# First chunk of a macaron FFN–attention–FFN kernel: GpSimd's root moved ahead of a weight piece, the turned weights in two banks by halves, the guard of the sums as a last column

## The chip, the cores and the metric

The kernel runs on one core of one Trainium2 chip. Its time is the device time of one execution in microseconds (us). The kernel before took 542.42 us (median of 3 runs, 542.03 to 543.43).

## The reference

The input x has 2048 tokens of 128 numbers. The layer is a "macaron": half a mixture-of-experts FFN, attention, and half an FFN again, with the same FFN weights both times.

```python
def _L0_attn_ref(x, Wq, Wk, Wv):              # D = 128
    q, k, v = x @ Wq, x @ Wk, x @ Wv
    score = softmax(q @ k.T, axis=-1) / sqrt(128)
    return score @ v

def _L0_ffn_ref(x, centroids, expert_biases, Ws_up, Ws_down, W_up, W_down):
    xf = x.reshape(T, D)                      # T = 2048, E = 64 experts, F = 64, TOP_K = 8
    shared = silu(xf @ Ws_up) @ Ws_down
    aff = xf @ centroids.T
    _, idx = top_k(aff + expert_biases, TOP_K)
    w = sigmoid(aff[idx])
    w = w / (sum(w, axis=-1) + 1e-08)         # the 1e-08 is the "guard" of the sums
    cw = zeros((T, E)).at[tokens, idx].add(w)
    h = silu(einsum('td,edf->etf', xf, W_up))
    y = einsum('etf,efd->etd', h, W_down)
    return shared + einsum('etd,te->td', y, cw)

x = x + 0.5 * ffn(layernorm(x));  x = x + attn(layernorm(x));  x = x + 0.5 * ffn(layernorm(x))
```

## The kernel before

Tokens are worked on in four chunks of 512 (`CH`), in each of the two FFNs; the chunk's number n runs from 0 to 7, and n = 0 is the first chunk of the first FFN. Every expert is computed for every token, two experts at a time: a chunk has 33 units, unit 0 (the shared expert) and units 1 to 32 (a pair of experts each, 128 hidden numbers).

A unit passes through the engines in this order. TensorE (PE) computes the hidden rows (`up`, L1201, three matmuls L1197 to L1199, since each fp32 operand is kept as a high and a low part). ScalarE (ACT) applies silu (L458). VectorE (DVE) multiplies by the gate, which is the token's weight for that expert spread over 64 partitions (`gate_unit`, L739). ACT makes the high part (L469), DVE or GpSimd (POOL) the low part (L296). PE multiplies by the down weights and accumulates (`down`, L1228, three matmuls L1239 to L1241), five units behind `up` (`LAG`).

The gates reach the partitions in two ways. Units 7 to 32 of chunk 0 get them by DMA: the turned weights are copied to the tile `gates` (L503), stored to memory (L335, queue of SyncE, SP), and read back with a broadcast, two DMAs of 128 KB to each unit (L358). Units 1 to 6 (`EARLY`) of the chunks 0 and 4 get them by a matmul with a selection matrix `sel` (`spread_gate`, L1226) from the turned weights `cwT`, since the store and the read back would come too late.

Before its first unit the first chunk needs its whole prologue: statistics, normalised tokens turned, affinities, the eight largest, sigmoid, the sum with its guard (`pro_sum`, L944), the reciprocal, the weights `cw2` (`first_weights`, L930), four transposes into one PSUM bank `mp` (`pro_cw`, L1325, matmuls L1302), and the copy of that bank to `cwT` (L597). PE fills two of its waits there with matmuls that nobody reads (`stay_awake`, L1415, L1418).

The expert weights arrive as 16 pieces (`raw`, L327), alternately of the up and the down weights. ACT makes the high part of a piece (`piece_hi`, L548, cast L550) and POOL the low part (`piece_lo`, L385, subtraction L387). All of this stands in written order: each engine's instructions run strictly in the order in which the program lists them, and wait for each other by semaphores; no scheduler moves them.

The next chunk's prologue runs inside a chunk. Of chunk 1's, POOL computes the inverse square root of the variances (`rstd`, L378: L382 and a power, L383) in chunk 0's unit 3, behind the pieces 3 and 4. DVE refines it (L773, L760 to L762), normalises the tokens in two pairs of tiles (L776, units 5 and 6), and PE turns them (L1309, unit 8).

The buffers: `hid` is four banks of `lrow`; `bank` is four banks, of which `mp` is the third and `mq` the fourth; `yacc` (the accumulator of `down`) is the first bank in even chunks.

## Time and profile before

| | us |
|---|---|
| median of 3 runs (lowest, highest) | 542.42 (542.03, 543.43) |
| the profiled execution's own time | 542.28 |
| its span (first to last instruction) | 540.5 |
| PE busy in the span | 532.0 |
| ACT, DVE, POOL busy | 406.6, 408.8, 272.6 |

The profiled execution is one of many; its span leaves out some 1.8 us at the two ends of it. The page gives busy times and the chain of work that ended last; further views of the same trace give the instructions in order of time, one engine at a time, the busy times in stretches, and for each group of DMAs the time from issue to landing. Times on the axis are us from the span's start. "[idle before <-X]" behind an instruction is how long its engine had nothing to do ahead of it, and what ended this. Matmuls are pipelined: a 128x512 one is shown as 0.40 us, but the next one starts 0.23 us behind it.

### The profile page before, as it was taken

Reading aid. Unit: us, or ns where it says so; the run is one execution under the profiler, and the core shown is the slowest. Engines: PE = TensorE matmul, PEld = TensorE weight load, DVE = VectorE, ACT = ScalarE, POOL = GpSimd, SP = SyncE. Lnnn points to the kernel's source line nnn. Section 1 sums busy time; section 2 is a strip of 40 time slices with the busy share of each in tenths; the row PEclk is TensorE's granted clock in tenths of the full one; section 3 lists DMA queues with packets and bytes.
Section 4 is the critical chain, followed back from the end, with each engine's and each line's share of the span. In section 5 each row is a group of like instructions: output and inputs, shape, how many; then the busy total and the mean of one; then the engine's idle time right before and its main releaser. Section 6 shows DMA issues by size and latency. Waiting matters only on the chain.

```text
span 540.5 us, 8719 instructions
## 1 busy us (share of the span) xinstructions
PE 532.0 (98%) x2710; PEld 437.2 (81%) x2710; DVE 408.8 (76%) x934; ACT 406.6 (75%) x815; POOL 272.6 (50%) x241
## 2 busy tenths in 40 slices
PE   8899999999999999999999999999999999999997
PEld 6577887887788888799999999878887888788886
DVE  6888679877975677867877889779668767965664
ACT  7798778877887775866666657778779777877773
POOL 2679657775776764000000000267576676766663
PEclk9999999999999999999999999999999999999999
DMA  8477564564566550000000000165565565657652
GB/s 270 137 228 217 180 203 161 178 198 149 174 191 195 183 172 1 2 1 0 1 2 1 2 1 0 44 193 169 168 198 165 168 201 166 187 156 204 204 191 84
DMA packets 44494, 72.25 MB, mean 134 GB/s; under 512 B 8864, under 2 KB 9888, under 8 KB 44448
## 3 DMA queue, kind: packets, MB, share of 16 engines
q1 hardware_dynamic: 44000, 71.37, 42.6%
q8 instruction: 21, 0.34, 0.3%
q10 hardware_dynamic: 448, 0.33, 0.2%
q14 instruction: 25, 0.20, 0.1%
HBM read 69.57 MB, written 2.10 MB: 133 GB/s over the span
## 4 chain that ended last, share of the span: by engine, by line
PE 89%; DVE 4%; ACT 2%; DMA 1%; issue 1%; POOL 1%; SPq 0%; DVEq 0%
PE lrow L1197 13%; PE lrow L1198 13%; PE lrow L1199 13%; PE bank L1239 10%; PE bank L1241 10%; PE bank L1240 10%; PE bank L1302 6%; PE bank L1526 3%; PE bank L1527 3%; PE bank L1528 3%; DMA wide<-gates_dram 1%; DVE pmax L982 1%; PE bank L1309 1%; DVE gpart_lo L296 1%; PE bank L1198 1%
## 5 line engine op out<-in xcount | busy, mean ns | idle before, releaser
L296 POOL TENSOR_TENSOR gpart_lo<-gated,gpart_hi 128x512 fp32r<-128x512 f32 x174 | 223.7, 1296 | 163.2 <-ACT gpart_hi L469 161.6
L458 ACT ACTIVATE lrow<-lrow 128x512 f32<-128x512 f32 (+1 forms) x245 | 143.8, 587 | 62.5 <-PE lrow L1199 62.0
L739 DVE TENSOR_TENSOR gated<-lrow,wide 128x512 f32<-128x512 f32 x170 | 116.2, 684 | 56.9 <-ACT lrow L458 53.4
L469 ACT CAST gpart_hi<-gated 128x512 fp32r<-128x512 f32 x174 | 106.6, 613 | 6.0 <-DVE gated L739 5.4
L1239 PE MATMUL bank<-gpart_lo,wdn_hi 128*128 128x512 f32 x246 | 97.8, 397 | 0.0
L1241 PE MATMUL bank<-gpart_hi,wdn_hi 128*128 128x512 f32 x246 | 97.7, 397 | 0.0
L1240 PE MATMUL bank<-gpart_hi,wdn_lo 128*128 128x512 f32 x246 | 97.2, 395 | 0.0
L739 DVE TENSOR_TENSOR lrow<-lrow,wide 128x512 f32<-128x512 f32 x74 | 51.5, 696 | 26.9 <-ACT lrow L458 26.9
L1115 DVE TENSOR_TENSOR pT_lo<-bank,pT_hi 128x512 fp32r<-128x512 f32 x64 | 43.7, 684 | 21.7 <-ACT pT_hi L671 21.7
L296 DVE TENSOR_TENSOR gpart_lo<-lrow,gpart_hi 128x512 fp32r<-128x512 f32 (+1 forms) x83 | 56.6, 682 | 1.5 <-ACT gpart_hi L469 1.3
L671 ACT CAST pT_hi<-bank 128x512 fp32r<-128x512 f32 x64 | 38.0, 594 | 24.2 <-PE bank L1302 24.0
L469 ACT CAST gpart_hi<-lrow 128x512 fp32r<-128x512 f32 (+1 forms) x83 | 49.1, 592 | 8.4 <-DVE lrow L739 8.2
L1239 PEld LDWEIGHTS bank<-gpart_lo,wdn_hi 128*128 128x128 f32 x246 | 46.2, 188 | 11.3
L1241 PEld LDWEIGHTS bank<-gpart_hi,wdn_hi 128*128 128x128 f32 x246 | 46.2, 188 | 11.1
L1240 PEld LDWEIGHTS bank<-gpart_hi,wdn_lo 128*128 128x128 f32 x246 | 46.2, 188 | 10.9
L664 ACT ACTIVATE prow<-lrow,nmax 128x512 f32<-128x512 f32 x63 | 43.6, 695 | 14.2 <-DVE nmax L987 14.2
L1197 PE MATMUL lrow<-xnT_lo_a,wup_hi 128*128 128x512 f32 x128 | 52.1, 407 | 1.2 <-DVE gpart_lo L296 0.6
L1197 PE MATMUL lrow<-xnT_lo_b,wup_hi 128*128 128x512 f32 x128 | 51.3, 401 | 0.2 <-DVE gpart_lo L296 0.2
L1199 PE MATMUL lrow<-xnT_hi_a,wup_hi 128*128 128x512 f32 x128 | 50.7, 396 | 0.0
L1198 PE MATMUL lrow<-xnT_hi_b,wup_lo 128*128 128x512 f32 x128 | 50.7, 396 | 0.0
L1198 PE MATMUL lrow<-xnT_hi_a,wup_lo 128*128 128x512 f32 x128 | 50.6, 395 | 0.0
L1199 PE MATMUL lrow<-xnT_hi_b,wup_hi 128*128 128x512 f32 x128 | 50.1, 392 | 0.0
(280 smaller groups left out, 977.3 us busy)
## 6 DMA issues: line engine op xcount, KB each, us to landing
wide<-gates_dram SPq DMA_DIRECT2D x488, 128.0 KB, 3.0
raw<-in_w_up SPq DMA_DIRECT2D x8, 256.0 KB, 4.8
raw<-in_w_down SPq DMA_DIRECT2D x8, 256.0 KB, 5.0
gates_dram<-gates SPq DMA_DIRECT2D x8, 128.0 KB, 2.2
x<-in_x SPq DMA_DIRECT2D x3, 256.0 KB, 4.5
out_dram<-x SPq DMA_DIRECT2D x3, 256.0 KB, 2.9
x<-in_x SPq DMA_DIRECT2D x1, 128.0 KB, 2.8
x<-in_x ACTq DMA_DIRECT2D x1, 128.0 KB, 3.0
```

Source lines behind the costliest of these rows:

```text
L296: return eng.tensor_tensor(gpart[1][0:m, U % NGP, :], gated_at(U)[0:m, :], gpart[0][0:m, U % NGP, :].bitcast(F32), ALU.subtract)
L458: nc.scalar.activation(dst[0:m, :], hid[U % NH][0:m, :], ACT.Silu).then_inc(s_silu, 1)
L469: nc.scalar.copy(gpart[0][0:m, U % NGP, :], gated_at(U)[0:m, :]).then_inc(s_ghi, 1)
L664: nc.scalar.activation(prow[:, j * CH:(j + 1) * CH], logit_bank(t, j), ACT.Exp, bias=nmax[:, t % 2:t % 2 + 1], accum_out=psums[:, t, j:j + ...
L739: nc.vector.tensor_tensor(gated_at(U), a, b, ALU.mult).then_inc(s_gated, 1)
L1115: nc.vector.tensor_tensor(pT[1][at], tb[q % 2][:, :].rearrange("p (k n) -> p k n", n=P), pT[0][at].bitcast(F32), ALU.subtract).then_inc(a_ ...
L1197: nc.tensor.matmul(out, a[0], b[1], start=True, stop=False)
L1198: nc.tensor.matmul(out, a[1], b[0], start=False, stop=False)
L1199: return nc.tensor.matmul(out, a[0], b[0], start=False, stop=True)
L1239: nc.tensor.matmul(y, w[0], g[1], start=(U % (NCH * PAIRS + 1) == 0), stop=False)
L1240: nc.tensor.matmul(y, w[1], g[0], start=False, stop=False)
L1241: nc.tensor.matmul(y, w[0], g[0], start=False, stop=(u == (UNITS - 1 if n % NCH < NCH - 1 else UNITS - LAG - 1))).then_inc(s_down, 1)
```

## The change

There are five edits, nearly all of them for chunk 0.

- POOL's `rstd` for chunk 1 moves from unit 3 to unit 0, ahead of weight piece 3 (the fourth) instead of behind the pieces 3 and 4.
- ACT's cast of weight piece 0 moves ahead of `make_sel` and of the cast of the shared down weights.
- The weights tile `rec` gets a 65th column in each of its four groups, set to 1e-8 once; the sum runs over 65 columns, and the addition of the guard (L948) is gone, in all eight chunks.
- Chunk 0's turned weights go to two banks, two transposes each (`mp` and `bank[0]`, columns 0 to 255). ACT copies the halves apart, with a semaphore of its own for the first, and PE's matmul of unit 1's gate runs in two halves, each behind its own copy. The copy to `gates` is in halves, too.
- The first `down`, which writes `bank[0]`, waits for the copy to `gates`. The wait for the whole of `cwT` ahead of chunk 0's unit loop goes, as the halves' waits stand in `spread_gate`.

```diff
--- before.py
+++ after.py
@@ -111,7 +111,8 @@
         stat = sb("stat", [P, 2, TPC, 6])
         mv = sb("mv", [P, 2, TPC, 2])
         rs = sb("rs", [P, 2, 4, TPC])
-        rec = sb("rec", [P, TPC, E])
+        rec_guard = sb("rec_guard", [P, TPC, E + 1])
+        rec = rec_guard[:, :, 0:E]
         sil = sb("sil", [P, TPC, E])
         rest = sb("rest", [P, TPC, E])
         top = sb("top", [P, TPC, TOP])
@@ -157,6 +158,7 @@
         s_x0b = sem("x_in0_second_half")
         s_small, s_sdn, s_value, s_qk, s_bias = (
             sem("small_in"), sem("shared_down_in"), sem("value_in"), sem("qk_in"), sem("bias_in"))
+        f_cwT, f_cwr = sem("first_cwT_half"), sem("first_cwT_half_read")
         s_eps, s_zero = sem("eps_made"), sem("cw_zeroed")
         j_out, j_aff, j_silu, j_hi, j_lo = (sem("shared_" + n) for n in ("and_aff", "aff_copied", "silu", "hi", "lo"))
         p_rec = sem("p_reciprocal")
@@ -410,6 +412,7 @@
                                     base=0, pattern=[[-1, P]], channel_multiplier=1).then_inc(s_id, 1)
             nc.gpsimd.memset(wsdn_pad[0:F, :].bitcast(F32), 0.0).then_inc(s_pad, 1)
             nc.gpsimd.memset(cw2[:, :, E:2 * E], 0.0).then_inc(s_zero, 1)
+            nc.gpsimd.memset(rec_guard[:, :, E:E + 1], 1e-8).then_inc(s_zero, 1)
             link(nc.gpsimd.memset(mhalf[:, :], -0.5))
             pool.wait_ge(s_small, 16 * 2)
             nc.gpsimd.tensor_copy(small[0][:, 0:E + F], raws[:, 0:E + F]).then_inc(s_wh0, 1)
@@ -426,10 +429,12 @@
                     for u in range(min(c, 1), UNITS):
                         if on_pool(place(u, n)):
                             low_part(nc.gpsimd, place(u, n)).then_inc(s_glop, 1)
+                        if n == 0 and u == 0:
+                            rstd(0, 1, p_st, p_rs)
                         if n == 0 and u % 2 == 0 and PRE + u // 2 < 2 * WP:
                             piece_lo(PRE + u // 2)
                         if c + 1 < NCH:
-                            if u == 3:
+                            if n and u == 3:
                                 rstd(0, n + 1, p_st, p_rs)
                             if u == 18:
                                 weights(n + 1)
@@ -500,7 +505,11 @@
                     nc.scalar.copy(cwT[:, :], mp[:, :]).then_inc(p_cwr, 1)
                 if n:
                     act.wait_ge(s_gout, 16 * n)
-                nc.scalar.copy(gates[:, :], mp[0:E, :]).then_inc(s_gates, 1)
+                if n:
+                    nc.scalar.copy(gates[:, :], mp[0:E, :]).then_inc(s_gates, 1)
+                else:
+                    nc.scalar.copy(gates[:, 0:GW], mp[0:E, 0:GW])
+                    nc.scalar.copy(gates[:, GW:CH], bank[0][0:E, 0:GW]).then_inc(s_gates, 1)
 
             def epi_y(n):
                 act.wait_ge(s_down, place(PAIRS, n) + 1)
@@ -580,11 +589,11 @@
                         if f == 0:
                             first_hi(0)
                             first_hi(1)
+                            piece_hi(0)
                             act.wait_ge(s_spread, 1)
                             make_sel()
                             act.wait_ge(s_sdn, 16 * 2)
                             nc.scalar.copy(wsdn[0][:, :], rawd[:, :]).then_inc(s_wh, 1)
-                            piece_hi(0)
                             piece_hi(1)
                             first_sil(0)
                             first_sil(1)
@@ -593,8 +602,9 @@
                             silu_unit(1, n)
                             hi_unit(0, n)
                             silu_unit(2, n)
-                            act.wait_ge(p_cwT, 1)
-                            nc.scalar.copy(cwT[:, :], mp[:, :]).then_inc(p_cwr, 1)
+                            for h in range(2):
+                                act.wait_ge((f_cwT, p_cwT)[h], 1)
+                                nc.scalar.copy(cwT[:, h * GW:(h + 1) * GW], (mp, bank[0])[h][:, 0:GW]).then_inc((f_cwr, p_cwr)[h], 1)
                             piece_hi(2)
                             silu_unit(3, n)
                             hi_unit(1, n)
@@ -944,9 +954,8 @@
             def pro_sum(n):
                 dve.wait_ge(p_w, n + 1)
                 total = (mp if n else bank[0])[:, TPC * E:TPC * E + TPC] if n != NCH else wsum[:, 0, :]
-                link(nc.vector.tensor_reduce(total, rec[:, :, :], AX, ALU.add))
-                link(nc.vector.tensor_scalar(wsum[:, 0, :], total, 1e-8, None, ALU.add))
-                nc.vector.reciprocal(inverse_sum(n), wsum[:, 0, :]).then_inc(p_inv, 1)
+                link(nc.vector.tensor_reduce(total, rec_guard[:, :, :], AX, ALU.add))
+                nc.vector.reciprocal(inverse_sum(n), total).then_inc(p_inv, 1)
 
             def epi_x(n, c):
                 dve.wait_ge(e_yT, n + 1)
@@ -1013,7 +1022,7 @@
                             first_lo(1)
                             first_top()
                             first_chosen()
-                            dve.wait_ge(s_zero, 1)
+                            dve.wait_ge(s_zero, 2)
                             first_weights(n)
                             small_lo(1, wsdn, rawd, 0, D)
                             lo_unit(0, n)
@@ -1223,6 +1232,13 @@
                     if u == EARLY and n:
                         pe.wait_ge(a_x, NQ)
                     one = sel[:, u - 1, :, :].rearrange("p e f -> p (e f)")
+                    if n == 0 and u == 1:
+                        for h in range(2):
+                            pe.wait_ge((f_cwr, p_cwr)[h], 1)
+                            half = slice(h * GW, (h + 1) * GW)
+                            ins = nc.tensor.matmul(gate_bank(u, n)[:, half], one, cwT[:, half], start=True, stop=True)
+                        ins.then_inc(s_gate, 1)
+                        return
                     nc.tensor.matmul(gate_bank(u, n), one, cwT[:, :], start=True, stop=True).then_inc(s_gate, 1)
 
             def down(u, n):
@@ -1232,6 +1248,7 @@
                     pe.wait_ge(s_w, 2 * ((u - 1) // (PAIRS // WP)) + 2)
                 if U == 0:
                     pe.wait_ge(s_wl, 2)
+                    pe.wait_ge(s_gates, 1)
                 wait_low(pe, U)
                 w = [a[:, u - 1, :] for a in wdn] if u else [a[0:F, :] for a in wsdn]
                 g = [a[0:m, U % NGP, :] for a in gpart]
@@ -1324,7 +1341,13 @@
 
             def pro_cw(n):
                 pe.wait_ge(p_cw, n + 1)
-                if n % NCH == 0:
+                if n == 0:
+                    for i in range(TPC):
+                        h, at = i // GT, i % GT * P
+                        ins = nc.tensor.transpose((mp, bank[0])[h][:, at:at + P], flat(cw2)[:, i * P:(i + 1) * P], ident[:, :])
+                        if i % GT == GT - 1:
+                            ins.then_inc((f_cwT, p_cwT)[h], 1)
+                elif n == NCH:
                     turn(flat(cw2), mp, p_cwT)
                 else:
                     for i in range(TPC):
@@ -1432,8 +1455,8 @@
                         stay_awake(2)
                         pro_cw(n)
                         stay_awake(1)
-                    if c == 0:
-                        pe.wait_ge(p_cwr, f + 1)
+                    if n == NCH:
+                        pe.wait_ge(p_cwr, 2)
                     for u in range(LEADS[1] if n == NCH else min(c, 1), UNITS):
                         if u <= EARLY and (c or u >= LEADS[f]):
                             up(u, n)
```

GpSimd's (POOL's) order in chunk 0, from the low part of weight piece 0 to that of piece 4; `wup_lo` and `wdn_lo` are low parts of weight pieces, `rs` is the root of the next chunk. Before:

```order
L387 TENSOR_TENSOR wup_lo<-raw,wup_hi 128x512
L387 TENSOR_TENSOR wdn_lo<-raw,wdn_hi 128x512
L387 TENSOR_TENSOR wup_lo<-raw,wup_hi 128x512
L387 TENSOR_TENSOR wdn_lo<-raw,wdn_hi 128x512
L387 TENSOR_TENSOR wup_lo<-raw,wup_hi 128x512
L382 TENSOR_SCALAR rs<-mv 128x4
L383 TENSOR_TENSOR rs<-rs,mhalf 128x4
```

And now:

```order
L389 TENSOR_TENSOR wup_lo<-raw,wup_hi 128x512
L389 TENSOR_TENSOR wdn_lo<-raw,wdn_hi 128x512
L389 TENSOR_TENSOR wup_lo<-raw,wup_hi 128x512
L384 TENSOR_SCALAR rs<-mv 128x4
L385 TENSOR_TENSOR rs<-rs,mhalf 128x4
L389 TENSOR_TENSOR wdn_lo<-raw,wdn_hi 128x512
L389 TENSOR_TENSOR wup_lo<-raw,wup_hi 128x512
```

The two instructions of the root moved ahead of two pieces.

ScalarE's (ACT's) order from the first high parts of the turned tokens to the copy to `gates`. Before:

```order
L566 CAST xnT_hi_a<-bank 128x256 x2
L555 CAST sel<-spread 128x768
L586 CAST wsdn_hi<-rawd 128x128
L550 CAST wup_hi<-raw 128x512
...
L458 ACTIVATE wide<-lrow 128x512
L597 CAST cwT<-bank 128x512
L550 CAST wup_hi<-raw 128x512
L458 ACTIVATE wide<-lrow 128x512
L469 CAST gpart_hi<-lrow 128x512
L503 COPY gates<-bank 64x512
```

And now:

```order
L575 CAST xnT_hi_a<-bank 128x256 x2
L559 CAST wup_hi<-raw 128x512
L564 CAST sel<-spread 128x768
L596 CAST wsdn_hi<-rawd 128x128
...
L463 ACTIVATE wide<-lrow 128x512
L607 CAST cwT<-bank 128x256 x2
L559 CAST wup_hi<-raw 128x512
L463 ACTIVATE wide<-lrow 128x512
L474 CAST gpart_hi<-lrow 128x512
L511 COPY gates<-bank 64x256
L512 COPY gates<-bank 64x256
```

The cast of the first weight piece moved up by two instructions, and the copies to `cwT` and to `gates` became two of half the columns each.

VectorE's (DVE's) order in chunk 0 from the chosen weights to the tile `cw` that PE turns. Before:

```order
L921 SCALAR_TENSOR_TENSOR rec<-rest,sil 128x256
L947 TENSOR_REDUCE bank<-rec 128x4
L948 TENSOR_SCALAR wsum<-bank 128x4
L949 RECIPROCAL bank<-wsum 128x4
L936 TENSOR_TENSOR rest<-rec,bank 128x4x12
```

And now:

```order
L931 SCALAR_TENSOR_TENSOR rec_guard<-rest,sil 128x4x64
L957 TENSOR_REDUCE bank<-rec_guard 128x4
L958 RECIPROCAL bank<-bank 128x4
L946 TENSOR_TENSOR rest<-rec_guard,bank 128x4x12
```

One instruction between the sum and the reciprocal is gone.

## Rows read from the trace of the kernel before

**Rows 1.** The page, part 1: busy us, share of the span, instructions

```profile
PE 532.0 (98%) x2710; PEld 437.2 (81%) x2710; DVE 408.8 (76%) x934; ACT 406.6 (75%) x815; POOL 272.6 (50%) x241
```

**Rows 2.** Stretches: length, each engine's busy us, clock, DMA share, GB/s

```profile
15.10:25.60 10.50, 8.59 (x33) 5.39 (x31) 9.04 (x24) 8.41 (x17) 7.50 (x7) 1.00 0.47 128
25.60:34.70 9.10, 9.10 (x41) 7.02 (x42) 7.22 (x12) 8.51 (x17) 7.41 (x6) 1.00 0.91 239
34.70:46.10 11.40, 10.99 (x48) 7.98 (x47) 11.27 (x30) 10.24 (x20) 8.57 (x8) 1.00 0.65 211
60.00:540.00 480.00, 476.68 (x2481) 396.29 (x2479) 361.31 (x809) 355.99 (x718) 233.40 (x199) 1.00 0.40 125
```

**Rows 3.** The chain that ended last, chunk 0: start us, us, what

```profile
8.80 1.30 POOL wup_lo L387
...
21.28 1.05 POOL rs L383
...
29.51 5.06 DMA wide<-gates_dram
```

**Rows 4.** ACT in order of time: start us, us, instruction, count, idle before

```profile
6.53 0.74 ACT L566 CAST xnT_hi_a<-bank 128x256 fp32r<-128x256 f32 x2
7.16 0.83 ACT L555 CAST sel<-spread 128x768 fp32r<-128x768 f32 x1
...
13.85 0.58 ACT L597 CAST cwT<-bank 128x512 fp32r<-128x512 f32 x1 [0.76 <-PE bank L1302]
...
16.33 0.58 ACT L503 COPY gates<-bank 64x512 f32<-64x512 f32 x1
```

**Rows 5.** L327 up to 12 us, twelve weight pieces: issue to landing

```profile
DMA to landing us min/median/max: 3.6/5.7/6.1
```

**Rows 6.** PE in order of time, 10 to 15 us

```profile
10.14 0.50 PE L1197 MATMUL lrow<-xnT_lo_a,wup_hi 128*128 128x512 f32 x1 [0.43 <-POOL wup_lo L387]
...
12.35 1.03 PE L1418 MATMUL bank<-ident 128*128 128x256 f32 x4
13.21 0.60 PE L1302 MATMUL bank<-ident,cw 128*128 128x128 f32 x4
...
14.49 0.50 PE L1226 MATMUL bank<-cwT,sel 128*128 128x512 f32 x1 [0.24 <-ACT cwT L597]
```

**Rows 7.** DVE in order of time, 11 to 16 us

```profile
11.71 0.16 DVE L948 TENSOR_SCALAR wsum<-bank 128x4 f32<-128x4 f32 x1
...
12.70 0.21 DVE L938 TENSOR_TENSOR cw<-cw,rest 128x48 f32<-128x48 f32 x1
...
15.12 0.69 DVE L739 TENSOR_TENSOR lrow<-wide,bank 128x512 f32<-128x512 f32 x1 [0.64 <-PE bank L1226]
```

**Rows 8.** DVE and PE in order of time, around chunk 1's normalised tokens

```profile
17.08 0.37 DVE L1029 BATCH_NORM_AGGREGATE mv<-stat 128x2 f32<-128x6 f32 x4
...
20.52 0.69 DVE L296 TENSOR_TENSOR gpart_lo<-lrow,gpart_hi 128x512 fp32r<-128x512 f32 x1
22.36 0.17 DVE L773 TENSOR_SCALAR bank<-mv 128x4 f32<-128x4 f32 x1 [1.15 <-POOL rs L383]
...
25.59 0.63 PE L1309 MATMUL bank<-ident,xn_a 128*128 128x128 f32 x4 [1.48 <-issue]
```

**Rows 9.** SP's store of the gates, and DVE at unit 13

```profile
16.94 0.51 SPq L335 DMA_DIRECT2D gates_dram<-gates  x1
...
34.66 0.69 DVE L739 TENSOR_TENSOR gated<-lrow,wide 128x512 f32<-128x512 f32 x1 [0.82 <-DMA wide<-gates_dram]
```

**Rows 10.** Issue to landing: eight of L358 from 22.95 on; the one at 29.51

```profile
DMA to landing us min/median/max: 3.4/3.7/3.9
...
DMA to landing us min/median/max: 5.1/5.1/5.1
```

**Rows 11.** DMA queues from 31.6 to 31.8 us: packets, MB, share of 16 engines

```profile
q8 instruction: 1, 0.02, 34.4%
```

**Rows 12.** PE in order of time, unit 17 of chunk 0

```profile
39.72 0.50 PE L1197 MATMUL lrow<-xnT_lo_a,wup_hi 128*128 128x512 f32 x1 [0.22 <-DVE gpart_lo L296]
```

## The prediction

> **What bounds the kernel now.** I read the page's busy times first: PE is busy 532.0 of 540.5 us [rows 1], so all that any edit can win is in PE's few gaps. The busy times by stretch say where they are: from 60 us on PE is busy 476.68 of 480.00, while from 15.1 to 25.6 it is busy 8.59 of 10.50 [rows 2]. The gaps that the change can reach are all in chunk 0's first 46 us. In that stretch the chain of waits, read third, goes from one engine to the next: POOL's low part of weight piece 0 at 8.80, the root for chunk 1 at 21.28, and from 29.51 a DMA of 5.06 us that brings the gates of unit 13 [rows 3]. Behind it DVE is the bound: from 34.7 to 46.1 it is busy 11.27 of 11.40 [rows 2], and PE waits for it, as at unit 18's `up` at 39.72 [rows 12]. So there are two sections with different limits: up to about 26 us the engines' own order, then the stream of gates, whose landing at 34.57 sets DVE free at 34.66 after an idle time of 0.82 [rows 9]. What is won ahead of 26 us counts only as far as this stream comes sooner too. That is the question of this case.
>
> **Part 1, weight piece 0 sooner.** ACT's cast of it takes the place of `sel` at 7.16 [rows 4] instead of coming two casts later; POOL's subtraction now starts at 8.80 [rows 3], the cast's end plus 0.07. The piece, issued at 2.58, landed 3.6 later at 6.2, the quickest of the twelve issued together [rows 5], so the cast finds its data. It and POOL come about 0.9 sooner. PE's first `up` matmul of unit 1 stands at 10.14 behind an idle time of 0.43 [rows 6]; with the step of 0.23 from the matmul before it and its start-up it could have stood at about 9.55. I take 0.59 for PE's own queue: the filler matmuls start at 11.76 instead of 12.35, and end 0.86 later at 12.62 [rows 6]. This alone gains nothing at 14.49; it only takes PE's filler out of the way of the transposes, which stood at 13.21 [rows 6] though `cw` was complete at 12.70 + 0.21 = 12.91 [rows 7].
>
> **Part 2, the guard.** L948 takes 0.16 and its place in the row 0.20 (11.71 to the reciprocal behind it) [rows 7]. The sum's row becomes 65 columns long, 4 of 256 elements more; I take nothing. `cw` is complete at 12.71. With PE free the transposes start about 0.1 later, at 12.83, instead of 13.21: a gain of 0.38 that needs both parts. The other seven L948 lie beside a PE that doesn't wait for them, and I take nothing; if one were on the path, it would be 0.20. The column stride of 65 instead of 64 changes reads that already ran in four groups; bound 0 to 0.05 each, taken 0.
>
> **Part 3, the halves.** The four transposes are shown as 0.60, two of them as about 0.38, so the first half can be copied at 12.83 + 0.38 + 0.04 = 13.25. Two 256-column casts take 0.74 as a pair against 0.58 for one of 512 [rows 4], so both are done at about 13.99 instead of 13.85 + 0.58 = 14.43. PE's second half of the gate starts at about 14.04 against 14.49, and being half as long ends 0.1 sooner still: unit 1's gating on DVE starts at about 14.57 instead of 15.12 [rows 7], a gain of 0.55. The cover is there: ACT sat idle 0.76 ahead of the copy [rows 4], and the filler behind the transposes ends before 14.04. The new wait of the first `down` for the copy to `gates` has behind it all of PE's queue, but PE gets there only after the gate of unit 5, which waits for DVE's gating of unit 3, and this stands behind the statistics of 17.08 [rows 8], now at about 16.9; the copy ends at about 16.5. Cost nothing.
>
> **Part 4, the copy to `gates`.** It follows the high part of unit 1, 0.55 sooner, and costs 0.16 more as two halves (0.74 against 0.58 again). The store, issued at 16.94 [rows 9], leaves at about 16.94 - 0.55 + 0.16 = 16.55. Gain 0.4.
>
> **Part 5, the root.** DVE's statistics end at 17.08 + 0.37 [rows 8], now some 0.55 sooner; POOL then needs 1.3 us for both instructions and is done at about 18.2, not 22.3. Nothing in POOL's queue behind it is late: the high part of piece 3 is the third instruction behind the copy to `gates` in ACT's queue, 16.33 + 3 x 0.48 + 0.62 = 18.4 by [rows 4], now 18.0, and finds POOL free at about 18.2. DVE had waited 1.15 for the root at 22.36 [rows 8]. Now it gets to L773 right behind its low part (20.52 + 0.69) [rows 8], and this is fed by ACT, 0.4 sooner: 20.8 instead of 22.36. PE's transposes of chunk 1's tokens follow by the same 1.55: 24.05 instead of 25.59 [rows 8]. So at 26 us the engines are 1.5 ahead.
>
> **Part 6, what is late next.** SP's stream of gates starts when the store has landed, and up to unit 13 no engine holds it: a unit's slot is free once the unit six before it is gated. It is 14 DMAs of 128 KB and 4 weight pieces of 256 KB long up to unit 13. From 25.6 to 34.7 the DMA engines are busy 0.91 of the time [rows 2]. So this stream comes 0.4 sooner, not 1.5. Its last DMA of unit 13 took 5.1 us, where the eight issued from 22.95 on took 3.4 to 3.9 [rows 10]; in this time an instruction fetch of 16 KB took a third of the 16 engines' 0.2 us, so 1.1 us of one of them [rows 11]. PE has the most instructions, so I take it for PE's; it then moves ahead with PE by some 1.3. It falls on the landing of unit 12 instead of 13, and its queue still carries most of the delay to unit 13. From this I take 0.1 more: unit 13 lands at about 34.07, and DVE, PE and the rest follow by 0.5. The other 1.0 is DVE waiting for gates in units 9 to 13.
>
> **The sum.** 0.55 - 0.16 + 0.1 = 0.5 us. The profiled execution would go from 542.28 to 541.8. The median of the runs shown is 0.14 above that execution: 542.42 - 0.5 = 541.9.
>
> **A rule weighed.** Behind `rec`, every tile declared later moves by 32 bytes in the partition, as the new tile has 1040 bytes and takes 1056; the tile `wide`, into which the gates are read back, moves from an address of 32 past a multiple of 64 to a multiple of 256. The Trainium skill (DMA: Bandwidth & Descriptors, How a descriptor splits into AXI transactions) says that a descriptor which doesn't start on a 256-byte boundary fetches from the boundary below it. By an estimate from this page a 2048-byte row of before would cost 71 beats of 32 bytes against 64 now, if the rule holds for the written side as well. No run here shows it yet.
>
> **The rivals.**
> A, the stream lets go. If unit 13 lands with 3.9 us like its forerunners, because the fetch falls elsewhere or the transfers of 128 KB get shorter with the tile's new address, it lands at 29.51 - 0.4 + 3.9 = 33.0, and DVE's idle 0.82 [rows 9] shows that it would have been ready at 33.84 and now at about 32.6 to 33. The gain is then 1.2 to 1.5 us, at the most the 1.55 of part 5: 540.9 to 541.2. For it: the 5.1 stands alone among its kind [rows 10]. Against it: DMA share 0.91 [rows 2], and the issues themselves are only 0.4 sooner. The rule of the Trainium skill above would work this way.
> B, nothing arrives. If the halves cost ACT more than they bring (each 0.37 and a wait), the store leaves where it left, and the stream with it. The gain of parts 1 to 3 and 5 is then all spent waiting for gates: 542.4.
> C, slower. The cast of weight piece 0 now stands ahead of `sel`, of the casts of the shared weights and piece 1, of the sigmoid and of a table load. If its transfer lands late, ACT stands. It has 1.0 us of room (6.2 against 7.16). Of the twelve weight pieces the slowest took 6.1 [rows 5]; with 6.1 here the cast starts at 8.7, 1.5 late, and the silus and the copy of `cwT` behind the table load come 1.5 later, less the 0.76 that ACT had idle [rows 4]. The gates leave 0.7 later instead of 0.4 sooner: 543.1. It decides from a landing of about 4.6 us on.
> That the change doesn't do what it says I see in none of its parts.
>
> **Chances.** The forecast 0.62 (own range 541.5 to 542.3), A 0.18, B 0.13, C 0.07. A measurement of this kernel tells about 0.3% from no change, 1.6 us: faster means below 540.8, slower above 544.0. Only the far end of A with some luck of the runs reaches below 540.8; I give it 0.10. Above 544.0 only C with a much later landing, 0.03. The rest, 0.87, is within. The range takes in the near end of A and most of C's, with the runs' own scatter of 542.03 to 543.43: 540.9 to 542.9.
>
> **What would show it.** Right: the four transposes of the weights from about 12.8, unit 1's gating at 14.6, the store at 16.55, DVE's L773 at 20.8 with no wait for the root, PE's transposes of chunk 1 at about 24.1, and in units 9 to 13 DVE waits for gates of 1.5 to 2 us in sum, where it had 0.82. Behind 46 us both kernels run alike, 0.5 apart. Wrong: if DVE waits less than 0.8 for gates up to unit 13, A is the case; if the store leaves at 16.9 or later, B; if ACT has a gap ahead of weight piece 0, C. If the two traces differ by more than a few tenths behind 60 us, something that I took at nothing (the stride, the addresses) isn't.

## The result and the profile after

The changed kernel takes 539.4 us in the median of 4 runs (538.99 to 539.7), the kernel before 542.22 in the same comparison. The ratio is 0.9943, with a 95% interval of 0.9926 to 0.996: faster by 0.6%. I had said 541.9 and 540.9 to 542.9, and gave a gain of over 0.3% a chance of one in ten. The profiled execution took 539.49 with a span of 537.7, 2.8 less than before.

The busy times of the page after, against [rows 1]:

```profile
PE 530.3 (99%) x2711; PEld 437.8 (81%) x2711; DVE 407.2 (76%) x926; ACT 407.1 (76%) x817; POOL 272.3 (51%) x242
```

The stretches after, columns as in [rows 2]:

```profile
15.10:25.60 10.50, 9.75 (x40) 6.39 (x39) 10.12 (x26) 9.32 (x20) 7.60 (x8) 1.00 0.46 148
25.60:34.70 9.10, 9.10 (x42) 7.02 (x40) 6.18 (x10) 8.35 (x17) 7.20 (x6) 1.00 0.72 221
34.70:46.10 11.40, 10.28 (x42) 7.26 (x41) 11.27 (x30) 10.10 (x20) 8.85 (x8) 1.00 0.68 212
60.00:540.00 480.00, 473.81 (x2477) 395.47 (x2475) 359.97 (x802) 356.12 (x717) 232.26 (x198) 1.00 0.39 124
```

From 15.1 to 25.6 PE works 1.16 us more than in [rows 2]; from 25.6 to 34.7 DVE works 1.04 less, since it waits. The last row is the surprise: 473.81 against the 476.68 of [rows 2], 2.87 less, though at 60 us PE is only 0.8 ahead and has no gap behind it to lose. The window's last 2.3 us lie behind the end of the changed kernel.

To find where the 2.8 us arise I set each matmul of the one trace against the same matmul of the other. The changed kernel is ahead by 0.31 us at the transposes of the weights, 0.52 at 15.06, 1.72 at 25.59, 1.34 at 36.5, 0.80 at 46.0 and 0.81 at 60. Then it gains steadily: 1.04 at 137, 1.29 at 207, 1.43 at 368, 1.92 at 431, 2.44 at 489, 2.80 at 531. So 0.8 us come from chunk 0 and 2.0 from stretches that the edited lines don't touch.

The first 26 us went as forecast. PE after, in order of time, against [rows 6] and [rows 8]:

```profile
11.76 1.03 PE L1441 MATMUL bank<-ident 128*128 128x256 f32 x4
12.90 0.66 PE L1347 MATMUL bank<-ident,cw 128*128 128x128 f32 x4
13.39 0.60 PE L1441 MATMUL bank<-ident 128*128 128x256 f32 x2
13.89 0.57 PE L1239 MATMUL bank<-cwT,sel 128*128 128x256 f32 x2
...
23.87 0.63 PE L1326 MATMUL bank<-ident,xn_a 128*128 128x128 f32 x4 [0.31 <-issue]
```

ACT after, against [rows 4], and the queue of SP, against [rows 9]:

```profile
7.33 0.62 ACT L559 CAST wup_hi<-raw 128x512 fp32r<-128x512 f32 x1
...
13.37 0.65 ACT L607 CAST cwT<-bank 128x256 fp32r<-128x256 f32 x2 [0.15 <-PE bank L1347]
...
15.81 0.36 ACT L511 COPY gates<-bank 64x256 f32<-64x256 f32 x1
16.07 0.37 ACT L512 COPY gates<-bank 64x256 f32<-64x256 f32 x1
16.47 0.51 SPq L337 DMA_DIRECT2D gates_dram<-gates  x1
```

DVE after, against [rows 7 to 9]:

```profile
12.64 0.21 DVE L948 TENSOR_TENSOR cw<-cw,rest 128x48 f32<-128x48 f32 x1
...
14.60 1.29 DVE L749 TENSOR_TENSOR lrow<-wide,bank 128x512 f32<-128x512 f32 x2 [0.18 <-PE bank L1239]
...
20.66 0.15 DVE L783 TENSOR_SCALAR bank<-mv 128x4 f32<-128x4 f32 x1
...
33.85 0.69 DVE L749 TENSOR_TENSOR gated<-lrow,wide 128x512 f32<-128x512 f32 x1 [1.40 <-DMA wide<-gates_dram]
```

The first gating of a unit with a gate starts at 14.60, the store leaves at 16.47, and the wait for the root (1.15 at 22.36 in [rows 8]) is gone. What was won is then spent waiting for gates. The waits of DVE up to 46 us (sum, times, longest), and the two transfers in the chain, which answer to the one in [rows 3]:

```profile
DVE gated L749 <- DMA wide<-gates_dram: 2.9, 3, 1.4
```
```profile
22.85 3.37 DMA wide<-gates_dram
...
28.91 4.85 DMA wide<-gates_dram
```

### The profile page after: what moved, and what is told of

It is laid out like the page before. It is cut to its first block, busy times and chain, and to the rows that moved or that the text cites. A ratio compares the mean times of both kernels' runs of the same rounds, so it can differ in the third digit from the quotient of the medians.

```text
span 537.7 us, 8716 instructions
## 1 busy us (share of the span) xinstructions
PE 530.3 (99%) x2711; PEld 437.8 (81%) x2711; DVE 407.2 (76%) x926; ACT 407.1 (76%) x817; POOL 272.3 (51%) x242
## 4 chain that ended last, share of the span: by engine, by line
PE 88%; DVE 5%; ACT 2%; DMA 2%; issue 1%; POOL 1%; POOLq 0%; DVEq 0%; SPq 0%; ACTq 0%
PE lrow L1206 12%; PE lrow L1208 12%; PE lrow L1207 12%; PE bank L1256 10%; PE bank L1258 10%; PE bank L1257 10%; PE bank L1319 5%; PE bank L1549 3%; PE bank L1551 3%; PE bank L1550 3%; DMA wide<-gates_dram 2%; PE bank L1441 1%; POOL gpart_lo L298 1%; DVE gpart_lo L298 1%; DVE pmax L991 1%
```

## Experiments on the part that nobody edited

Two theories at first: the new tile `rec_guard` is 32 bytes longer and shifts every tile declared behind it, and that speeds up the steady stretches; or something in the new code does. Times are medians; each ratio is to runs of the kernel before on the same chip (542.0 to 542.6 in all studies). An "interval" is the mean time from the start of a matmul to the start of the next in one profile, over pairs that stand side by side in both traces, gaps over 260 ns left out: 46 to 190 us is the first FFN, 190 to 340 attention, 340 to 515 the end of attention and the second FFN. Before they are 221.5, 138.0 and 216.2 ns, after 220.8, 137.8 and 214.5. (From 355 us on, without the end of attention, the last figure would be 223.1 before and 221.2 after.)

**Only the shift.** `+ sb("pad", [P, 8])` behind `rec` in the kernel before.

> The kernel before, with an unused tile of 32 bytes declared behind rec: no instruction is added, removed or moved, only every tile declared later stands 32 bytes further, as in the changed kernel. What is measured of the change is 2.8 us, of which PE shows 0.8 at 46 us and the rest growing steadily through the two FFNs (0.43 us between 46 and 190, 1.34 between 355 and 515), with no gap of PE getting shorter. Theory Addresses: the steady part comes from the tiles' addresses; this kernel then gains about 2.0 us (540.2), with nothing won ahead of 46 us but perhaps some tenths in the stream of gates. Theory Phase (the steady part comes from the order in which the engines meet, which the edits of chunk 0 have shifted): this kernel stays within 0.3 us of before (542.2).

Measured: 540.33 (539.48 to 540.99), ratio 0.9964 (0.9952 to 0.9977). The profile is 1.96 us ahead at 531 us, and 0.04 behind at 60. The code as it was, with the shift alone, gives the steady part.

**Only the code.** The changed kernel with 224 unused bytes more, so that the tiles start as before modulo 256.

> The changed kernel with an unused tile of 224 bytes behind the guarded tile, so that every later tile stands 256 bytes further than in the kernel before and has the same remainder modulo 256 as there. Theory Addresses: it keeps what is won ahead of 46 us, 0.8, and loses the steady part of 2.0: 541.4. Theory Phase: it keeps all, 539.4.

Measured: 541.76 (540.34 to 542.51, 11 runs), ratio 0.9986 (0.9976 to 0.9997); no drift behind 60 us (0.22 behind the kernel before at 60, 0.24 at 531). So the shift is the cause, and the theory of the new code falls. By the median the edited code alone is worth some 0.1%, and the forecast of 0.5 us lies in the interval; its profiled execution, with 542.51 the slowest of the eleven, shows none of it at 46 us.

**Which tile.** One or two unused tiles ahead of `wide`, `xnT_a` or `gpart` bring some to a multiple of 256 and leave those ahead of them. Within the FFN the tiles behind a second one (all behind `wide` in the first kernel, `gpart` in the last) don't start as before, though: their start is the same modulo 64, but modulo 256 it is 32 instead of 224.

```
wide only:        + sb("pad", [P, 8], F32, ffn)    ahead of wide, and again behind it
all but wide:     + the same behind wide; + sb("pad_b", [P, 8]) ahead of pT
gpart only:       + the same ahead of gpart, and again behind it
all but gpart:    + the same ahead of xnT_a, and again ahead of gpart
```

> The kernel before with 32 bytes ahead of the tile wide and 32 behind it: wide, into which SyncE's DMAs read the gates back, starts at a multiple of 256 bytes, and every later tile of the FFN stays at 32 past a multiple of 64, as before. Theory Written side: the gain of the 32 bytes (1.8 us of the kernel before in the first study) comes from the DMAs' writes into wide, whose 2048-byte rows no longer straddle a 64-byte line at both ends; this kernel then has all of it, 540.3. Theory Read side (tiles that PE, DVE and ScalarE read and write, gpart above all): it has none, 542.1.

> The counterpart: wide stays where it was (32 past a multiple of 64), and the 32 bytes stand behind it, so that the turned tokens, gated, gpart and all the rest of the FFN, and the attention's tiles, start at multiples of 256. Theory Written side: no gain, 542.1. Theory Read side: all of it, 540.3. If both kernels have a part, the tiles share the effect.

Measured: with `wide` alone 541.71, ratio 1.0 (0.9991 to 1.0009); with all but `wide` 540.48, ratio 0.9971 (0.996 to 0.9981). The target of the DMAs doesn't matter. With that falls the rule of the Trainium skill (DMA: Bandwidth & Descriptors, How a descriptor splits into AXI transactions) as an explanation here: the rows of `wide` then begin at a multiple of 256 bytes, and no time is won. This kernel isn't a clean test, since `xnT_a` and `gpart` moved by 64 bytes (intervals 222.2 and 215.4); the clean one is its counterpart, which has the gain without `wide`.

> The kernel before, in which only gpart_hi and gpart_lo (the moving operands of the matmuls with wdn) begin at a multiple of 256 bytes; every other tile of the FFN keeps a start of 32 modulo 64, and so do pT and its neighbours. Theory G (what counts are the starts of the moving operands that TensorE streams all the time): 540.3 to 540.8, a steady interval between matmuls in the second FFN near 214.5 ns against 216.2. Theory D (what counts are the tiles that VectorE, ScalarE and GpSimd read and write, gated above all, since gated goes with every second unit): 541.9 to 542.2, interval 216.2 ns. Theory S (each tile has its share): 541.2 to 541.6.

> The complement: xnT_a, xn_a, biased_a, aff_a, gated, yT and xn2 begin at a multiple of 256 bytes, gpart_hi and gpart_lo at 32 modulo 256 (as every tile before was 32 modulo 64). Theory G: 541.9 to 542.2, no gain in the second FFN, where the only moving operands besides gpart are xnT_b, which did not move. Theory D: 540.3 to 540.8. Theory S: 541.2 to 541.6.

Measured: `gpart` alone 540.77, ratio 0.9973 (0.9961 to 0.9984), intervals 221.6, 137.9, 214.7; all but `gpart` 541.25, ratio 0.9978 (0.9969 to 0.9987), intervals 220.8, 137.9, 215.6. So the second FFN goes by `gpart` nearly alone and the first by a tile from `xnT_a` to `xn2`. By the totals the first fits Theory G (540.3 to 540.8) and the second Theory S (541.2 to 541.6), so none of the three holds for both; by stage the split is sharper than any of them said: where `gpart` is what moves, the second FFN's interval falls by 1.5 ns also for the `up` matmuls that read `xnT_b`, which didn't move (230.3 against 233.5 for the low part of the weights). So the start of one operand also shows in the matmuls beside it in PE's row. What none of the theories explains: in the first FFN, where the same `gpart` is read as often, its start changed nothing (221.6 with it alone moved; 220.8 with the others moved, whether it stood at 0 or at 32).

**Which start.** 96, 160 and 224 unused bytes behind `rec`, in place of 32.

> The kernel before with 96 bytes behind rec instead of 32: wide and all behind it start at a multiple of 64, but not of 256 (64 past it). If the boundary that counts is 64 bytes, the gain is that of 32 bytes, 540.3. If it is 256 bytes, as the Trainium skill's rule on descriptors (DMA: Bandwidth & Descriptors, How a descriptor splits into AXI transactions) would have it, there is no gain or a small one, 541.7 to 542.1.

> The kernel before with 160 unused bytes behind rec: all tiles behind it (xnT_a, gated, gpart, pT) begin at 128 modulo 256. So far the steady interval between matmuls went with the start of the tile that TensorE reads: in the first FFN by xnT_a's start 220.8 ns at 0, 221.5 at 64, 222.2 at 32, 221.5 at 224; in the second FFN by gpart's 214.5 at 0, 215.2 at 64, 215.5 at 32, 216.2 at 224; in attention by pT's 137.8 at 0, 136.6 at 64, 137.9 at 224. Theory 1 (the start modulo 128 or 64 decides, and 128 does as 0 does): 540.3, intervals 220.8, 214.5, 137.8. Theory 2 (the place relative to other operands decides, so that each start modulo 256 or more has a value of its own): any total from 539.8 to 542.2, and intervals that don't repeat those of 0. Theory 3 (no system, chance of one execution): intervals near 221.5, 216.2, 138.0.

> The same with 224 unused bytes: all begin at 192 modulo 256. Theory 1: as at 64 modulo 256, so 540.6 with intervals 221.5, 215.2 and 136.6 (attention 1.1 us shorter than before). Theory 2: again values of their own. Theory 3: 542.1, 221.5, 216.2, 138.0.

Measured: 96 bytes 540.58, ratio 0.9975 (0.9966 to 0.9983); 160 bytes 536.02 (534.97 to 536.25), ratio 0.9882 (0.9868 to 0.9895); 224 bytes 538.13, ratio 0.9928 (0.9916 to 0.9941). From the first I took a boundary of 64 bytes for the rule, since the total was that of 32 bytes; the intervals already spoke against it, and the second refuted it. Every earlier theory missed 536.0 by 4 us. Theory 2 named the mechanism, not the size: its range ended at 539.8.

**The start itself, or the place relative to others.** The 160 bytes, and 128 more ahead of `x`, the first tile.

> The kernel before with 160 unused bytes behind rec, as in the kernel that took 536.0, and 128 more ahead of x, so that every tile lies 128 bytes further: the weights, xnT_b, qT, kT and v at 0 modulo 256, and xnT_a, gpart and pT at 0 too. If only the place of one tile relative to the others counts (all with the same remainder): 536.0, intervals near 216.4 ns in the first FFN and 211.6 in the second. If 128 modulo 256 itself is the good start: the first FFN as at 0 (220.8) or worse, the second between 214.5 and 216, total 540 to 542.

Measured: 535.13 (534.49 to 535.81), ratio 0.9867 (0.9854 to 0.9881), intervals 216.5, 137.4, 211.6, those of the 160 bytes to 0.1 ns. All tiles now begin at 0 modulo 256, where `gpart` and `xnT_a` alone had given 214.5 and 220.8. So it is the place relative to tiles ahead of `rec` that counts. In one row for each place (start less that of the weights `wup` and `wdn`, modulo 256), with the interval in ns (160 on: `wide` only, and all but `gpart`):

| tile behind `rec` begins | first FFN (`xnT_a`) | attention (`pT`) | second FFN (`gpart`) |
|---|---|---|---|
| 96 on (before) | 221.5 | 138.0 | 216.2 |
| 128 on (after) | 220.8 | 137.8 | 214.5 |
| 160 on | 222.2 | | 215.5 |
| 192 on (96 bytes) | 221.5 | 136.6 | 215.2 |
| 0 (160 bytes) | 216.4 | 137.5 | 211.6 |
| 64 on (224 bytes) | 218.2 | 136.6 | 215.2 |

How it looks in the profile: the two FFN stretches of the kernel before, with 32 bytes, with 160, and with 160 and 128, columns as in [rows 2]. PE is busy in all but 0.15 us of each; only the number of its matmuls in the stretch grows, from 712 to 727 in the second FFN.

```profile
46.00:190.00 144.00, 143.96 (x644) 115.87 (x645) 110.95 (x257) 114.72 (x218) 104.40 (x92) 1.00 0.57 184
355.00:515.00 160.00, 160.00 (x712) 128.52 (x711) 117.30 (x246) 126.66 (x239) 106.66 (x89) 1.00 0.61 182
```
```profile
46.00:190.00 144.00, 143.86 (x646) 116.38 (x646) 111.40 (x259) 114.90 (x219) 104.90 (x92) 1.00 0.57 185
355.00:515.00 160.00, 160.00 (x718) 129.77 (x718) 117.99 (x245) 127.41 (x241) 107.38 (x89) 1.00 0.60 183
```
```profile
46.00:190.00 144.00, 143.85 (x657) 117.66 (x656) 113.26 (x266) 115.98 (x221) 106.30 (x92) 1.00 0.60 187
355.00:515.00 160.00, 160.00 (x727) 131.71 (x726) 118.98 (x246) 128.88 (x243) 108.74 (x91) 1.00 0.60 185
```
```profile
46.00:190.00 144.00, 143.85 (x656) 117.49 (x655) 112.99 (x266) 116.23 (x221) 106.25 (x92) 1.00 0.59 187
355.00:515.00 160.00, 160.00 (x727) 131.71 (x726) 118.91 (x246) 129.00 (x243) 108.73 (x91) 1.00 0.61 186
```

And PE in order of time, second FFN, before and with 160 bytes. The start of one matmul after the other moves from steps of 0.23 or 0.24 to 0.22 or 0.23:

```profile
399.71 0.39 PE L1240 MATMUL bank<-gpart_hi,wdn_lo 128*128 128x512 f32 x1
399.94 0.40 PE L1241 MATMUL bank<-gpart_hi,wdn_hi 128*128 128x512 f32 x1
400.18 0.40 PE L1197 MATMUL lrow<-xnT_lo_b,wup_hi 128*128 128x512 f32 x1
```
```profile
401.05 0.39 PE L1241 MATMUL bank<-gpart_hi,wdn_lo 128*128 128x512 f32 x1
401.27 0.39 PE L1242 MATMUL bank<-gpart_hi,wdn_hi 128*128 128x512 f32 x1
401.50 0.39 PE L1240 MATMUL bank<-gpart_lo,wdn_hi 128*128 128x512 f32 x1
```

## Experiments on chunk 0

**The root.** Back at unit 3 in the changed kernel (e3), and, the other way round, moved alone in the kernel before (e4):

```
 e3:  -   if n == 0 and u == 0:
      -       rstd(0, 1, p_st, p_rs)
      -   if n and u == 3:          +   if u == 3:
 e4:  the same lines, the other way, in the kernel before
```

> The changed kernel with GpSimd's root for chunk 1 back behind the pieces 3 and 4. By my sum the root is what gets PE's transposes of chunk 1 1.55 sooner, but the stream of gates then takes all but 0.5 to 0.8. DVE waits for the root again, by about 0.9 (piece 4 ends 0.1 to 0.4 sooner than before, the low part 0.5). If the gates' stream decides, as forecast, chunk 0 is no longer than 0.3 us above the changed kernel's, since the landing of unit 13 doesn't depend on the root. Rival: the root is worth its wait, and it costs 0.7 to 1.0 us. Theory Addresses: the steady 2.0 stays either way, 539.4 to 540.3. Theory Phase: it can go anywhere between 539.4 and 542.

> The kernel before with only GpSimd's root ahead of piece 3. The gates leave no sooner (the store at 16.94 as before), so by the forecast's step on the stream unit 13 lands at 34.5 and nothing is won but what the shift of the instruction fetch brings: 0 to 0.3 us (542.0). Rival: the root alone brings PE forward for good, 0.8 us or more (541.4). Theory Addresses: no steady gain, as no tile moves. Theory Phase: some steady gain, 539.5 to 541.5.

Measured: without the early root 539.71 (539.18 to 540.14), ratio 0.9952 (0.994 to 0.9965); the early root alone 542.35, ratio 1.0001 (0.9992 to 1.001). The profile of the second, of an execution of 543.05, shows where it goes: PE is 1.07 ahead at 25.59 and 0.79 behind at 46. Its waits up to 46 us:

```profile
DVE gated L741 <- DMA wide<-gates_dram: 2.2, 2, 1.3
DVE lrow L741 <- DMA wide<-gates_dram: 1.2, 2, 0.9
```

Without the early root DVE waits 0.24 at unit 13 instead of 1.40, and is no later there:

```profile
33.49 0.69 DVE L747 TENSOR_TENSOR gated<-lrow,wide 128x512 f32<-128x512 f32 x1 [0.24 <-DMA wide<-gates_dram]
```

**The other parts.** The halves undone (one bank and one copy, as before); and, in another kernel, piece 0 and the guard undone, with 32 unused bytes in the guard's place.

> The changed kernel, in which only the two banks by halves are undone: the turned weights go through one bank, cwT and gates are copied whole. Piece 0 ahead, the guard as a last column, the early root and the addresses stay. If the halves give their full 0.55 us of the start on to the store of the gates, and through the stream of gates to the end (what I predicted): 539.9 to 540.1, store of the gates 0.5 later, unit 13's rows landing near 34.3. If the stream of gates does not carry it on: 539.4 to 539.6.

> The changed kernel with two parts undone, piece 0 ahead and the guard as a last column (its sum is a separate addition again); 32 unused bytes keep every address of the changed kernel. The halves and the early root stay. Halves and root have been worth 0 each when undone alone (539.4 and 539.7 against 539.4). If piece 0 and the guard carry the whole gain of the first chunk: 540.2 to 540.5, that of the kernel before with 32 unused bytes. If the parts stand in for each other, since the stream of gates lets only one of them through: 539.4 to 539.8.

Measured: without the halves 539.39 (539.35 to 540.07), ratio 0.9951 (0.9938 to 0.9963); without piece 0 and guard 539.9 (539.32 to 540.08), ratio 0.9956 (0.9943 to 0.997). With all parts undone (the 32 bytes alone) it was 0.9964. No part taken away singly changes more than the intervals leave open. That the stream lets only so much through can't be the reason here, as the store left no later in either profile: at 16.42 without the halves and 16.53 without piece 0 and the guard, against 16.47 with all parts. Without the halves:

```profile
12.63 0.66 PE L1306 MATMUL bank<-ident,cw 128*128 128x128 f32 x4
14.60 1.29 DVE L744 TENSOR_TENSOR lrow<-wide,bank 128x512 f32<-128x512 f32 x2 [0.45 <-PE bank L1230]
```

From the first transpose to the first gating it is 1.97 us here, 1.91 in all eleven profiles with the chunk's start as before, and 1.70 with the halves, so the halves do save 0.2 to 0.3. But `cw` was complete at 12.57, against 12.85 in the changed kernel, and the code of before gives 12.60 to 13.03 from one profile to the next. The scatter of single executions hides each part; what each is worth in the total stays open. At 46 us it is larger still: nine kernels with the code of before and other addresses were between 0.59 ahead and 0.10 behind it, and the edited code with the old addresses was 0.22 behind, where the changed kernel was 0.80 ahead.

**The stream itself.** `FIRST = 14` in place of 12: two more of the 256 KB weight pieces are loaded at the start, and no longer between the gates (the texts on record of the last versions call them units).

> The changed kernel with 14 weight pieces instead of 12 loaded ahead of the stream of gates (the buffer has room for 14), so that two DMAs of 256 KB, 1.2 us of issues and transfer, leave the stream between 18.9 and 34 us. Theory: in chunk 0 the stream of gates is what PE waits for through DVE, which in the changed kernel waits 2.9 us for gates ahead of 46 us; unit 13's gates then land 1.2 sooner, and 0.8 to 1.2 us are won on the changed kernel: 538.4. Rival: DVE is the bound by itself once the wait is gone, or the two pieces ahead make the prologue's loads late: 0 to 0.3 us, 539.3.

Measured: 538.54 (538.12 to 538.78), ratio 0.9938 (0.9926 to 0.995); at 46 us 1.66 ahead instead of 0.80. The interval of the ratio overlaps that of the changed kernel, so the times don't show the gain by themselves. The profiles do: the four with 14 pieces (this one and the next three) are 1.23 to 2.32 ahead at 46 us, the five of the edited code with 12, parts undone or not, between 0.22 behind and 1.03 ahead. DVE's waits for gates:

```profile
DVE gated L749 <- DMA wide<-gates_dram: 1.4, 1, 1.4
```

**The best version, in two steps.** First `FIRST = 14` and 64 unused bytes ahead of `pT`; the same with the root back; and then 128 bytes more behind `rec_guard`.

> The changed kernel with 14 units ahead of the first stream (FIRST = 14 in place of 12), and 64 unused bytes ahead of pT, so that pT_hi, pT_lo and prow begin at 64 modulo 256, as in the kernel with 96 unused bytes, whose attention ran 1.1 us shorter than before. If the three gains add (538.5 with 14 units, and 0.9 from pT's start): 537.6 to 537.9. If that attention's gain was chance of one execution, or came from another tile (qT, kT and v did not move there): 538.4 to 538.7.

> The version with 14 units ahead of the stream and pT at 64 modulo 256 (537.35), with the root back at unit 3. If the early root only pays once the stream of gates no longer bounds the first chunk (which would explain why it was worth nothing with 12): 537.9 to 538.4. If the root is worth nothing there either: 537.2 to 537.6.

> The changed kernel with 14 units ahead of the stream, 128 unused bytes behind rec_guard (FFN tiles at 128 modulo 256) and 64 ahead of pT (attention's tiles at 192). If the gains add, 536.0 less the first chunk's 1.8 (540.3 to 538.5) less attention's 0.8 (interval 136.6 ns against 137.5): 533.2 to 533.8. If a faster FFN shows other engines or the stream as the next bound: 534 to 535.5.

Measured: 537.35 (536.98 to 537.48), ratio 0.9907 (0.9894 to 0.9921); with the old root 538.31 (538.22 to 538.42), ratio 0.9927 (0.9915 to 0.994). The first is a little below what I had expected for gains that add (537.6 to 537.9). With 14 pieces the early root looks worth something: 1.0 us by the medians, 0.7 by the profiles (1.93 ahead at 46 us, with the old root 1.23). The intervals of the two comparisons still overlap a little (0.9915 to 0.9921), and 0.7 is within the scatter of single profiles, so this points to it and doesn't prove it. Last, 532.73 (532.24 to 532.94), ratio 0.9822 (0.9808 to 0.9835): 9.4 us less than before, and less than my 533.2 to 533.8. Its profile is 2.32 ahead at 46 us and 9.70 at 531; of the attention's gain only part came along (interval 137.0; in 537.35 it was 136.9), so `pT` and the tiles behind it don't carry all of the 136.6.

## Why the prediction was wrong

- **Parts 1 and 2** held: fillers at 11.76 as said, transposes at 12.90 (said 12.83), a gain of 0.31 for 0.38; `cw` was complete at 12.85 instead of 12.71, since the sum itself started 0.13 later in this execution (11.38 for 11.25).
- **Part 3** held: gating at 14.60 (said 14.57). Its 0.55 is what parts 1 to 3 give together: 0.31 is the transposes, 0.21 the halves. The text on record for the run without the halves takes all of it for theirs. **Part 4**: store at 16.47 (said 16.55). **Part 5**: L783 at 20.66 with no wait (said 20.8), PE's transposes at 23.87 (said 24.05).
- **Part 6** had the right mechanism: 1.72 us ahead shrink to 0.80, DVE waiting 2.9 us for gates in three waits (said 1.5 to 2 in sum). The term was 0.5 and measured 0.8: the last DMA of unit 13 left 0.6 sooner (28.91 for 29.51) instead of 0.4, and took 4.85 for 5.06, 0.2 less instead of 0.1. Against the scatter above that is no difference, and that it came so near is in part luck: the same code with the old addresses was 0.22 behind at 46 us in its profile, with 5.72 for that DMA. Its median of 11 runs, 0.1% below the kernel before, is the better evidence for the 0.5. Part 5 brings nothing on its own, as part 6 implies.
- **The step that failed** is an edit that I took at nothing: the 32 bytes by which all tiles behind `rec` move. I had seen it, and weighed it only for the DMAs into `wide`, where it is worth nothing. It was 2.0 of the 2.8 us (1.8 by the medians of the shift alone, 540.33 against 542.13), in TensorE's steady interval, which I had not thought could change: "Behind 46 us both kernels run alike". The last sentence of the prediction named the sign to look for, and it came.
- **Rivals.** A gave 540.9 to 541.2 by a stream that lets go; the stream didn't. B and C didn't occur: the store left sooner, and ACT's cast of piece 0 at 7.33 had no idle ahead of it.

## What to carry to other kernels

A change of a tile's size is a change of all addresses behind it, and it can be worth more than the edit: compare kernels with the same starts, or undo the shift with an unused tile, before believing in a gain or loss of some tenths of a per cent. In a stretch where TensorE is always busy, count its matmuls; here up to 2.3% of their interval hung on where the tiles begin, and that costs one line to try. What is won ahead of a saturated stream can be spent waiting for it: the early root alone gave nothing, and seemed to pay only when the stream was shortened. And one profile of each kernel doesn't tell parts of 0.2 us from each other, where the same code scatters by more.

## What the runs showed of the hardware that I had not expected

The interval between matmuls with nothing to wait for went from 221.5 to 216.4 ns in the first FFN and from 216.2 to 211.6 from 340 to 515 us (means over all pairs, some of them of fewer columns) by the tiles' starts alone. For the six kinds of 512-column matmuls from 355 to 515 us it was 230.0 to 235.6 before and 226.6 to 227.7 with 160 bytes. All were at 2.4 GHz (granted clock 1.00 in the rows above). Best in both FFNs were tiles with the same start modulo 256 as the weights; in attention 64 bytes before or after was best (136.6 against 137.5). What collides is open. Among the tiles that stayed are the weights, which PE reads in its loads, `xnT_b`, `v` and `x`; in the first FFN PE doesn't read `xnT_b`, which points to the weights, but no run moved the weights alone. The Trainium skill (SBUF — State Buffer, Who interferes with whom) says that PE never waits on anyone, and that its two read ports, for the moving operand and for the weight load, are independent. By that nothing could meet, yet the interval hung on the starts. The runs don't tell two accesses of PE itself from traffic of DVE, ACT and POOL, since each tile that moved is also written by one of them.
